# Sums added straight into the result tensor: x1 and the expert outputs of a graph and expert layer, on one core

## The reference

```
x = x + _L0_gnn_ref(_layernorm(x, axis=-1), edge_index, edge_type_8, ...)        # "x1" in the kernel
x = x + _L0_ffn_ref(_layernorm(x, axis=-1)[None], gate_w, w1, w2, w3)[0]

# _L0_ffn_ref, for its N = 1250 rows:
scores = jax.nn.softmax(x @ gate_w.T, axis=-1)
top_scores, sel = jax.lax.top_k(scores, 2)              # two of 8 experts for each row
...                                                     # rows sorted by expert, y = SwiGLU of that expert
weighted = y * scores_sorted[:, None]
out = jnp.zeros((N, D), x.dtype).at[tok_sorted].add(weighted)
```

## Time and profile before

| | |
|---|---|
| median of 3 runs | 1808.44 us (1805.97 to 1808.8) |
| the profiled execution | 1806.31 us |
| its span in the trace | 1804.6 us, so 1.7 us lie around it |
| mean granted TensorE clock | 0.973 |
| PE busy | 94% of the span |

### The profile page before, as it was taken

One profiled execution on the slowest core, in us unless ns is written; L12 is line 12 of the kernel. 1 busy time (PEld: TensorE's weight loads), 2 busy tenths in 40 slices (PEclk: granted clock), 3 DMA queues, 4 the chain that ended last, 5 costly groups with the idle time before them and its releaser, 6 DMA issues. The chain is left out here.

```text
span 1804.6 us, 22163 instructions
## 1 busy us (share of the span) xinstructions
PE 1698.9 (94%) x7873; PEld 1402.6 (78%) x7873; DVE 1095.6 (61%) x1490; ACT 727.8 (40%) x1230; POOL 770.8 (43%) x663
## 2 busy tenths in 40 slices
PE   7999999999999999999999999999789948999993
PEld 5888888888888888888787878878678846878882
DVE  8554656664564342424499999999799876333200
ACT  2315665541231213122266665656511204554551
POOL 1002222225775656502256655656265515455531
PEclk9999999999999999999999999999899958999997
DMA  5336555556324444343699888888734437867545
GB/s 207 94 117 221 176 162 177 187 159 228 100 82 142 133 129 141 120 149 123 243 331 317 268 308 286 290 301 273 264 133 171 149 124 228 234 172 222 129 90 153
DMA packets 141051, 339.70 MB, mean 188 GB/s; under 512 B 19332, under 2 KB 35764, under 8 KB 140864
## 3 DMA queue, kind: packets, MB, share of 16 engines
q1 hardware_dynamic: 90128, 179.00, 29.3%
q0 software_dynamic: 50816, 159.29, 29.0%
HBM read 241.19 MB, written 102.15 MB: 190 GB/s over the span
## 5 line engine op out<-in xcount | busy, mean ns | idle before, releaser
L1054 POOL DMA_INDIRECT gathered<-Y,edge_row x184 | 234.1, 1272 | 178.8 <-PE banks L1213 137.1
L625 ACT ACTIVATE ghi<-gathered,edge_w 128x1024 fp32r<-128x1024 f32 x184 | 211.3, 1152 | 138.8 <-DMA gathered<-Y,edge_row 93.4
L1030 POOL DMA_INDIRECT edge_w<-INV,edge_key x184 | 207.9, 1130 | 119.9 <-DMA edge_w<-INV,edge_key 88.0
L1071 PE MATMUL banks<-whi,xhi 128*128 128x512 f32 x640 | 252.5, 395 | 0.6 <-DVE xlo L768 0.6
L945 DVE SCALAR_TENSOR_TENSOR glo<-gathered,edge_w,ghi 128x1024 fp32r<-128x1024 f32 x184 | 235.4, 1279 | 25.3 <-ACT ghi L625 23.2
L1073 PE MATMUL banks<-whi,xlo 128*128 128x512 f32 x640 | 249.5, 390 | 0.0
L1072 PE MATMUL banks<-wlo,xhi 128*128 128x512 f32 x640 | 249.5, 390 | 0.0
L1212 PE MATMUL banks<-ghi,sel 128*128 128x512 f32 x368 | 145.3, 395 | 10.3 <-DVE glo L945 10.0
L575 ACT ACTIVATE ring_hi<-raw_chunk 128x512 fp32r<-128x512 f32 x112 | 66.5, 624 | 207.5 <-PE banks L1175 134.3
L1213 PE MATMUL banks<-glo,sel 128*128 128x512 f32 x368 | 143.4, 390 | 0.0
L1071 PEld LDWEIGHTS banks<-whi,xhi 128*128 128x128 f32 x640 | 120.5, 188 | 25.4 <-DVE xlo L768 1.2
(11 more groups left out here) (316 smaller groups left out, 3683.9 us busy)
## 6 DMA issues: line engine op xcount, KB each, us to landing
raw<-in_L_ffn_w SPq DMA_DIRECT2D x24, 1024.0 KB
Y<-y_out SPq DMA_DIRECT2D x80, 256.0 KB
t_set<-in_L_gnn_weight POOLq DMA_DIRECT2D x64, 256.0 KB
TW<-t_set POOLq DMA_DIRECT2D x64, 256.0 KB
raw_chunk<-TW SPq DMA_DIRECT2D x64, 256.0 KB
w_stage<-in_L_gnn_weight SPq DMA_DIRECT2D x30, 512.0 KB, 5.0
raw_chunk<-in_L_gnn_weight SPq DMA_DIRECT2D x48, 256.0 KB
Y<-half_v SPq DMA_DIRECT2D x40, 256.0 KB
```

The costliest lines, as they stand in the source:

```text
L625: nc.scalar.activation(ghi[:, t % HR], gath[t % GR][:], ACT.Copy, scale=edge_w[:, t:t + 1]).then_inc(g_hi, 1)
L1030: nc.gpsimd.indirect_dma_start(out=edge_w[:, t:t + 1], out_offset=None, in_=INV, in_offset=bass.IndirectOffsetOnAxis(ap=edge_key[:, t:t + ...
L1054: nc.gpsimd.indirect_dma_start(out=gath[t % GR][:], out_offset=None, in_=Y, in_offset=bass.IndirectOffsetOnAxis(ap=edge_row[:, t:t + 1], a ...
L1071: pe.matmul(psum[slot][:], xhi[:, k, at], whi[h][:, k], start=(k == 0), stop=False)
```

## The change

The scratch tensor `X1` goes. `x1` is stored straight into the result (its last tile with 98 rows), the additions go into the result, and the copy behind the last addition is dropped. The result has no spare rows, so the lanes without a token have to be sent (with their zeros) to rows of the result, and within one addition no row may be named by such a lane that also gets a real sum. For that DVE marks which of rows 0 to 127 are in the last tile of each expert (`in_last`, `spare[:, 0]`) and keeps for each expert and lane p the row p + 1 where it is not in that tile, else 0 (`spare[:, 1]`). PE turns this matrix into bank 6, DVE takes the largest row of each expert (`some_row`), PE spreads it to all lanes, and DVE uses it where `spare[:, 1]` is 0. `pad_row` then picks for each of the 28 columns of `add_i` the row of that tile's expert. PE waits for `score_ready` before it first writes bank 6 with an output.

```diff
-                    sp.dma_start(X1[d * P:(d + 1) * P, :], x1[:, d % 2]).then_inc(x1_out[d % 2], 16)
-                    if d == 0:
-                        sp.dma_start(X1[NP:NP + P, :], x1[:, 0]).then_inc(x1_out[0], 16)
+                    sp.dma_start(out[d * P:d * P + rows(d), :], x1[:rows(d), d % 2]).then_inc(x1_out[d % 2], 16)
...
                 sp.wait_ge(ye_out[0], 16 * ((MT + 1) // 2))
                 sp.wait_ge(ye_out[1], 16 * (MT // 2))
-                for j in range(0, NT, 2):
-                    at = slice(j * P, min(N, (j + 2) * P))
-                    sp.dma_start(out[at, :], X1[at, :]).then_inc(out_stored, 16)
-                sp.wait_ge(out_stored, 16 * (NT // 2))
...
-                        out=X1, out_offset=bass.IndirectOffsetOnAxis(ap=add_i[:, i:i + 1], axis=0),
+                        out=out, out_offset=bass.IndirectOffsetOnAxis(ap=add_i[:, i:i + 1], axis=0),
...
+                step(v.tensor_scalar(last_at[:], ce[:, 2, :], -float(P), None, ALU.add))
+                step(v.tensor_tensor(in_last[:], wit[:, :, 0:2], last_at[:].unsqueeze(2).to_broadcast([P, X, 2]),
+                                     ALU.is_ge))
+                step(v.tensor_tensor(in_last[:], in_last[:], oh_e[:, :, 0:2], ALU.mult))
+                step(v.tensor_reduce(spare[:, 0, :], in_last[:], AX.X, ALU.add))
+                step(v.tensor_scalar(lane_row[:], lanes[:], 1.0, None, ALU.add))
+                v.tensor_scalar(spare[:, 1, :], spare[:, 0, :], 0.5, lane_row[:], ALU.is_lt,
+                                ALU.mult).then_inc(rt_poh, 1)
+                dve.wait_ge(rt_placed, 1)
...
-                step(v.tensor_scalar(lane_row[:], lanes[:], float(NP + 1), None, ALU.add))
+                dve.wait_ge(rt_placed, 2)
+                step(v.tensor_reduce(some_row[0:X, P:P + 1], psum[6][0:X, P:2 * P], AX.X, ALU.max))
+                v.tensor_copy(some_row[0:X, 0:P], some_row[0:X, P:P + 1].to_broadcast([X, P])).then_inc(rt_poh, 1)
                 step(v.tensor_tensor(score[:, 0], psum[7][:, MTE:2 * MTE], score[:, 1], ALU.add))
-                step(v.tensor_scalar(add_s[:, 0], psum[7][:, 0:MTE], 0.5, lane_row[:], ALU.is_lt, ALU.mult))
+                step(v.tensor_tensor(pad_row[:], te[:, 1, :].unsqueeze(2).to_broadcast([P, MTE, X]),
+                                     iota[:, 0:X].unsqueeze(1).to_broadcast([P, MTE, X]), ALU.is_equal))
+                dve.wait_ge(rt_placed, 3)
+                step(v.scalar_tensor_tensor(spare[:, 2, :], spare[:, 1, :], 0.5, psum[6][:, 2 * P:2 * P + X],
+                                            ALU.is_lt, ALU.mult))
+                step(v.tensor_tensor(spare[:, 2, :], spare[:, 2, :], spare[:, 1, :], ALU.add))
+                step(v.tensor_tensor(pad_row[:], pad_row[:], spare[:, 2, :].unsqueeze(1).to_broadcast([P, MTE, X]),
+                                     ALU.mult))
+                step(v.tensor_reduce(add_s[:, 1], pad_row[:], AX.X, ALU.add))
+                step(v.scalar_tensor_tensor(add_s[:, 0], psum[7][:, 0:MTE], 0.5, add_s[:, 1], ALU.is_lt, ALU.mult))
...
-                ins.then_inc(rt_tok, 1)
+                ins.then_inc(rt_placed, 1)
+                pe.wait_ge(rt_poh, C2 + 1)
+                pe.transpose(psum[6][0:X, P:2 * P], spare[:, 1, :], ident[:]).then_inc(rt_placed, 1)
+                pe.wait_ge(rt_poh, C2 + 2)
+                pe.matmul(psum[6][:, 2 * P:2 * P + X], some_row[0:X, 0:P], ident[0:X, 0:X],
+                          start=True, stop=True).then_inc(rt_placed, 1)
...
                             pe.wait_ge(ye_evac[c], i)
+                        elif c == 1:
+                            pe.wait_ge(score_ready, 1)
```

More of the change, by code:

```diff
@@ L120, in build_program @@
         XN2 = dram("XN2", (NP, D))
-        X1 = dram("X1", (NP + P, D))
         def rows(j):
@@ L1318, in _ @@
                 for i in range(2):
-                    sp.wait_ge(x1_out[i], 16 * (NT // 2 + (i == 0)))
+                    sp.wait_ge(x1_out[i], 16 * NT // 2)
                     sp.wait_ge(xn2_out[i], 16 * NT // 2)
@@ L1418, in finish @@
                     if j >= 2:
-                        dve.wait_ge(x1_out[i], 16 * (j // 2 + (i == 0)))
+                        dve.wait_ge(x1_out[i], 16 * (j // 2))
                         dve.wait_ge(xn2_out[i], 16 * (j // 2))
@@ L1554, in build_program @@
         lane_row = z5.put("lane_row", [P, 1], F32)
+        last_at = z5.put("last_at", [P, X], F32)
+        in_last = z5.put("in_last", [P, X, 2], F32)
+        spare = z5.put("spare", [P, 3, X], F32)
+        some_row = z5.put("some_row", [P, P + 1], F32)
+        pad_row = z5.put("pad_row", [P, MTE, X], F32)
         add_s = z5.put("add_s", [P, 2, MTE], F32)
@@ L1559, in build_program @@
         first_tile = z5.put("first_tile", [P, X], I32)
-        rt_lg, rt_exp, rt_oh, rt_tot, rt_rank, rt_poh, rt_tok, rt_idx, rt_ready = (
+        rt_lg, rt_exp, rt_oh, rt_tot, rt_rank, rt_poh, rt_placed, rt_idx, rt_ready = (
             sem("shifted_logits_ready"), sem("exp_done"), sem("expert_onehot_ready"), sem("expert_totals_done"),
-            sem("expert_ranks_done"), sem("token_onehots_ready"), sem("tokens_placed"), sem("token_index_ready"),
+            sem("expert_ranks_done"), sem("token_onehots_then_spare_rows_ready"), sem("tokens_then_pad_rows_placed"), sem("token_index_ready"),
             sem("tile_expert_ready"))
@@ L1602, in build_program @@
         assert HC == 2 and 2 * H == BANK
-        score_ready, out_stored = sem("scores_placed"), sem("out_stored")
+        score_ready = sem("scores_placed")
         with nc.Block() as block:
@@ L1816, in _ @@
                                     ALU.is_equal).then_inc(rt_poh, 1)
-                dve.wait_ge(rt_tok, 1)
+                step(v.tensor_scalar(last_at[:], ce[:, 2, :], -float(P), None, ALU.add))
[7 more added lines that the diff above has]
+                dve.wait_ge(rt_placed, 1)
                 step(v.tensor_scalar(tok_s[:], psum[7][:, 0:MTE], -1.0, 0.0, ALU.add, ALU.max))
```

## The result

The changed kernel takes 1789.4 us in the median of 4 runs (1786.11 to 1792.4), the kernel before 1807.91 us in the median of 4; the ratio is 0.9899, with a 95% interval of 0.9879 to 0.9918. Two more timings of the same kernel gave 0.9922 (0.9909 to 0.9936) and 0.9908 (0.9894 to 0.9922). The profiled execution took 1789.49 us, with a span of 1787.7 us: 16.9 us less than before.

The account below looks back on a forecast made before the run. TensorE, busy 94% of the span, was taken as the bound, except at the end, where the copy ran alone. -17.7 + 0.5 = -17.2 us gave 1789.1 to 1791.2, forecast 1790.5 us, range 1787.0 to 1794.5.

Parts of the forecast that it names:

- (c): Six added DVE instructions ahead of `tok_s`, partly filling an idle wait for PE: +0.5 us, ends 0 and 1.8 us.
- (a): Copy at the kernel's end leaves the path in full: -17.7 us, at least the waiting alone, -14.5 us.
- rival 4: End of program has a cost that the copy hid: only 14.5 us gained, 1793.7 us; 5 in 100.
- (b): Dropping tile 0's second store lets SP fetch tile 2's `xr` 0.47 us sooner: taken as 0, at most 1.06 us.
- (d): DVE work added between `tok_i` and `add_i`: expert 0's weight splits 3.1 us later, hidden with 2.6 us slack left; 0 us.
- (e): Two small PE matmuls and a wait ahead of `turn_x(0)`, within PE's idle time before the first gather lands: 0 us.
- (f): The 27 additions go to result rows with as many bytes, lanes possibly sharing `some_row`: no difference taken.
- Rival 1: Additions into the result are slower: 1 us each gives +2 us, 2.7 us cancels the gain; 9 in 100.
- Rival 2: TensorE's clock falls otherwise behind the first SwiGLU wait, 1.5 us spared or incurred: 1789 or 1792 us; 10 in 100.
- Rival 3: Weight splits come 7 us later, not 3.1, so PE waits 1.3 us: 1791.8 us; 4 in 100.

Follow-up runs that it names:

- spare_last: The kernel before with only the second store of tile 0 (to the spare rows) moved behind the last store of the gate block; 0.9999 (0.999 to 1.0008).
- no_copy: The kernel before with only its final copy taken out, the result left unwritten; 0.9912 (0.9899 to 0.9926) of the kernel before.
- dve_later: The changed kernel with three 128x2048 memsets on VectorE between the score's sum and `pad_row`; 0.993 (0.9916 to 0.9943) of the kernel before.
- pool_waits: The changed kernel with GpSimd waiting for its own last addition at the end; profiled, span ends 4.7 us behind the landing instead of 2.3.
- pool_busy2: The changed kernel with two 128x1024 additions on GpSimd behind its last DMA; profiled, drain over at 1791.66 us, 4.5 us behind GpSimd's last operation.
- pool_busy1: The changed kernel with one 128x1024 addition on GpSimd behind its last DMA; profiled, drain ends at 1791.6 us, 2.3 us behind the landing.

## Why the prediction came out as it did

The time (1789.4 us against 1790.5) and the sign were right, and so was the cause: the copy lay on the path and left it. The sum of -17.2 us met the 16.9 us of the traces by errors that cancel: the last stretch gave 2.4 us less than I had for the copy (2.0 of it the drain's doing, the rest a last addition that landed in 6.4 us instead of 5.9), the stretch ahead of tile 0's end cost 1.4 us, (c) cost 0.3 us less, and 3.3 us were won where I had nothing. That the number came out so near is luck. Two signs that I had set came out against me: the span ended 2.3 us behind the last landing and not within 1 us, and the gate block changed its length by 1.3 us, more than the 1 us beyond which I had called myself wrong.

- **(a), the copy.** The step that failed is "I exclude that a part remains: no engine has work in the stretch". The busy times of a stretch don't list a queue's own waiting, and GpSimd's drain was in it for 2.2 us (1786.54 to 1788.76). The copy gave 15.7 us, not 17.7. This was rival 4 in kind, which I gave 5 in 100, with 14.5 us for its size.
- **(b), the second store.** I priced it at 0, having followed the wait to the one that takes its place; that reading was right. What I left out is that GpSimd also started from `xn`, and that VectorE's product then waits for the rest of GpSimd's running operation. It gave 1.3 us, which `spare_last` shows by itself.
- **(c), ahead of `tok_s`.** +0.2 us, against +0.5. The six instructions took 1.15 us from start to start and not 1.34; the reduction of 16 elements is no dearer than the others (0.20 to the next start), and the last one, 0.23 us long, has its follower start 0.14 us behind its own start.
- **(d), ahead of the splits.** The first split came 2.64 us later on the clock of the trace, 2.5 without the shift of the block, against 3.1, and 2.9 us of cover were left, against 2.6. Nothing of it showed. That `minus` is the first thing to run out of cover I had not seen. The first split for expert 1, which I put at about 1511, came at 1506.07, sooner than the 1507.73 of before: SP issued the load 2.6 us later, but it was there 9.8 us behind its issue instead of 14.1. Why it was quicker is open.
- **(e)** cost nothing, as said.
- **(f), additions into the result.** Median 7.6 and 7.7 us to landing in the changed kernel and 7.4 into `X1` (`no_copy`), and 37.7 us of waiting ahead of additions where it was 41.8 and 41.0; the last one took 6.4 us to land, and 5.9 (before) and 6.3 (`no_copy`) into `X1`. No price that could be told. Rival 1 does not hold; its part about shared rows was not put to the test, since by the inputs each expert has 300 to 328 rows and rows 0 to 127 always come first in its list, never in its last tile, so every lane without a token has a row to itself. An addition in which such lanes share a row was not tried.
- **Rival 2, the clock**, was right in kind and size: 1.5 us, with either outcome in one and the same program. The Trainium skill's sentence on it (TensorE: Matmul & The Clock Gate, "What's actually happening") agrees with that. No run shows that the start of the gathers decides it, as I had supposed.
- **Rival 3** didn't come about; `dve_later` shows where it would.

On the Trainium skill's rule for the copy (DMA: Bandwidth & Descriptors, "Anatomy of one DMA"), an estimate of 13.7 us: the copy took 17.6 to 17.7 us, so the row was the better price for its length, and neither named what it hid. The page gives that rule for DMAs that GpSimd issues; these were SP's.

## What to carry to other kernels

A stretch at the end in which no engine is busy is not yet free to remove in full: look at how each queue leaves the block, for what is being hidden under the last transfer. When a transfer is taken away or moved, follow not just the wait that it causes but every engine that starts sooner, since an operation may have to wait for what another engine is doing when it starts: the wait here was 1.06 us, and the product came out 1.18 us shorter. And compare two executions stretch by stretch, with a repeat of the unchanged program beside them: here 1.5 us of a gain of 2 us were TensorE's clock, which the change had not brought.

## What the runs showed of the hardware

GpSimd's queue ends this block by a DRAIN that is over at the later of its last operation or wait + 4.5 us and the landing of its last indirect DMA + 2.0 to 2.3 us (14 traces of 11 kernels; the first decides in `pool_waits` and `pool_busy2`, the two meet in `pool_busy1`, the second decides in the others). Why it takes these times is open. Having it wait for its own DMA lengthened the end from 2.3 to 4.7 us behind the landing. VectorE's 128x1024 product `th` of two SBUF tensors took between 1.22 and 3.41 us: 1.22 or 1.23 with GpSimd idle (as at 1449 us in the trace of before), and else until 1.07 to 1.17 us behind the end of the GpSimd operation, itself on two SBUF tensors, that ran when it started. The 128-row addition of half rows (2 KB) landed in 4.6 us, that of whole rows in 5.9 to 6.5 us at the quiet end, while GpSimd needed 1.57 us for either.
